# Two attentions and a mixture of experts on one core: the cosine shift in the score product, rotary halves on VectorE, idle products between chunks, narrow value units side by side

## The reference

```python
xn = _layernorm(x, axis=-1)
x = x + _L0_attn_ref(xn, Wq, Wk, Wv, g_scale) + _L0_ffn_ref(xn, g1, g2, wq, ...)

# _L0_attn_ref: 16 heads of 8 columns, cosine attention, no mask
q, k = _l2norm(q), _l2norm(k)
scores = g_scale * einsum('bhqd,bhkd->bhqk', q, k)
out = einsum('bhqk,bhkd->bhqd', softmax(scores), v)

# _L0_ffn_ref: 16 query heads, 4 key/value heads, rotary positions, causal
q = q * cos + _rotate_half(q) * sin        # k the same, then repeated
scores = where(causal, einsum('bhqd,bhkd->bhqk', q, k) / sqrt(8), -inf)
x = x + (softmax(scores) @ v) @ wo         # of the RMS-normed input
x = x + moe(rmsnorm(x))                    # 4 experts, top 2, hidden 384
```

## Time and profile before

| | us |
|---|---|
| median of 3 runs | 691.45 |
| lowest, highest | 690.83, 691.85 |
| profiled execution, its time | 691.39 |
| its span, first to last instruction | 689.7 |
| PE busy in the span | 631.6 |
| ACT busy | 479.7 |
| DVE busy | 361.7 |
| GpSimd busy | 110.5 |

### The profile page before, as it was taken

How to read it: one execution, slowest core, us unless ns; L and a number is a source line. 1 busy time by engine, 2 the same in 40 slices (tenths; PEclk the granted TensorE clock), 3 DMA queues, 4 the chain that set the end, 5 groups by cost and what they waited for, 6 DMA issues and landing times.

```text
span 689.7 us, 11207 instructions
## 1 busy us (share of the span) xinstructions
PE 631.6 (92%) x4138; PEld 284.3 (41%) x4138; DVE 361.7 (52%) x1037; ACT 479.7 (70%) x521; POOL 110.5 (16%) x257
## 2 busy tenths in 40 slices
PE   7758889999999999999999999999998789999996
PEld 6433333333333333333333333333333445566654
DVE  6586875565555555556455554553611434343333
ACT  1457868898898898889889889888997332222221
POOL 4488002102100200210210031021011200000000
PEclk8886999999999999999999999999999899999999
DMA  3002113214022120316302122030000000000000
GB/s 86 1 7 41 26 26 59 31 17 64 2 46 36 29 47 7 59 23 162 56 10 47 25 39 47 3 62 1 1 3 1 0 1 0 17 1 15 1 15 16
DMA packets 17525, 19.50 MB, mean 28 GB/s; under 512 B 6720, under 2 KB 14144, under 8 KB 17472
## 3 DMA queue, kind: packets, MB, share of 16 engines
q1 hardware_dynamic: 15072, 18.50, 15.2%
q10 hardware_dynamic: 2400, 0.30, 0.3%
HBM read 3.84 MB, written 1.05 MB: 7 GB/s over the span
## 4 chain that ended last, share of the span: by engine, by line
PE 74%; DVE 11%; ACT 8%; POOL 2%; issue 2%; DMA 1%; SPq 0%; DVEq 0%; ACTq 0%; POOLq 0%
PE ps L1197 25%; PE ps L1178 18%; PE ps L1292 6%; ACT probs L698 6%; PE ps L1278 6%; PE ps L1279 5%; PE ps L1123 5%; PE ps L1147 3%; DVE neg_piece L836 2%; DVE masked_scores L832 2%; DVE out_t L915 2%; PE ps L1140 1%; PE ps L1136 1%; DMA x_tok<-in_x 1%; PE ps L1089 1%
## 5 line engine op out<-in xcount | busy, mean ns | idle before, releaser
L698 ACT ACTIVATE probs<-ps,cos_shift 128x1024 f32<-128x1024 f32 x256 | 269.8, 1113 | 29.6 <-PE ps L1178 27.5
L701 ACT ACTIVATE probs<-ps 128x1024 f32<-128x1024 f32 (+2 forms) x160 | 144.7, 940 | 29.0 <-PE ps L1178 27.6
L832 DVE CUSTOM_DVE_ANT_0 masked_scores<-ps,mask_q 128x384 bf16<-128x384 f32 (+3 forms) x256 | 111.7, 488 | 73.7 <-PE ps L1123 73.0
L1197 PE MATMUL ps<-probs,v_cos_pad 128*32 128x512 f32 x1024 | 137.7, 610 | 0.0
L1178 PE MATMUL ps<-q_cos_t,k_cos_t 64*128 64x512 f32 x512 | 123.8, 482 | 5.0 <-ACT probs L698 3.9
L592 POOL TENSOR_SCALAR_AFFINE_SELECT probs<-probs 128x512 f32<-128x512 f32 x64 | 40.3, 635 | 404.2 <-ACT probs L701 404.2
L1178 PEld LDWEIGHTS ps<-q_cos_t,k_cos_t 64*128 64x128 f32 x512 | 48.2, 186 | 127.6 <-ACT probs L698 91.2
L739 ACT ACTIVATE probs<-ps 128x512 f32<-128x512 f32 x48 | 28.5, 597 | 96.3 <-PE ps L1279 84.9
L836 DVE TENSOR_REDUCE neg_piece<-ps 128x1 f32<-128x512 f32 x128 | 82.2, 684 | 22.8 <-PE ps L1123 22.8
L1197 PE MATMUL ps<-probs,v_causal_pad 128*32 128x512 f32 (+3 forms) x768 | 81.6, 498 | 0.3 <-POOL probs L592 0.3
L1123 PE MATMUL ps<-k_causal_t,q_causal_t 33*128 33x512 f32 (+3 forms) x384 | 64.4, 373 | 16.2 <-DVE neg_piece L836 9.0
(11 more groups left out here) (142 smaller groups left out, 458.1 us busy)
## 6 DMA issues: line engine op xcount, KB each, us to landing
q_causal_t<-parts_t_rope SPq DMA_DIRECT2D x64, 64.0 KB
q_cos_t<-parts_t_cos SPq DMA_DIRECT2D x56, 64.0 KB
k_cos_t<-parts_t_cos SPq DMA_DIRECT2D x28, 64.0 KB
k_cos_t<-parts_t_cos SPq DMA_DIRECT2D x56, 32.0 KB
parts_cos<-in_w SPq DMA_DIRECT2D x2, 768.0 KB, 5.7
x_tok<-in_x SPq DMA_DIRECT2D x4, 256.0 KB, 4.4
k_causal_t<-parts_t_rope SPq DMA_DIRECT2D x16, 64.0 KB
k_causal_t<-parts_t_rope SPq DMA_DIRECT2D x32, 32.0 KB
```

The source lines that it names most:

```text
L698: act.activation(step_probs(n), step_scores(n), ACT.Exp, bias=cos_shift[:, :])\
L701: act.activation(step_probs(n), step_scores(n), ACT.Exp).then_inc(probs_ready, 1)
L832: ins = dve.tensor_tensor_reduce(out=masked_scores[:, head % 2, at:at + keys], in0=scores, in1=mask_q[:, BANK - keys:BANK], scale=-1.0, sc ...
L1197: ins = pe.matmul(acc[32 * h:32 * h + 32, lo:], v, unit_probs(n)[:, h, lo:], start=j == 0, stop=True, skip_group_check=True)
```

## The change

1. *Cosine layout.* Each of the four heads gets 64 rows of its own in the keys (`k_cos_t` is twice as wide: two heads per half). 32 rows are the products; in two more, the queries hold the shift (rounded part and rest) and the keys hold 1. The exponential of the cosine steps has no bias any more. For the first group the constant rows are added when ACT and DVE copy the chosen rows (four copies each, three before); for later ones GpSimd fills the tiles once.
2. *Rotary halves.* DVE writes the second rotary halves, GpSimd no longer does.
3. *Unread products.* Six ahead of the projection of chunks 1, 2 and 3; six, not four, before the first scores.
4. *Narrow causal units.* The value unit of 256 columns moves one step later, to the step of the unit of 128 columns.
5. Score step 3 waits for DVE's copies (step 4 before).

```diff
@@ constants and the table of value units
-EARLY_WARM_UP, WARM_UP = 28, 4
+EARLY_WARM_UP, BETWEEN_CHUNKS, WARM_UP = 28, 6, 6
...
+    for n, (kind, half, j) in enumerate(UNITS * iters):
+        if kind == CAUSAL and j == half * CT + 2:
+
+            at[n] = at[n + 1]
     return at
...
-        k_cos_t = [sb(f"k_cos_t{i}", [P, SEQ]) for i in range(2)]
+        k_cos_t = [sb(f"k_cos_t{i}", [P, 2, SEQ]) for i in range(2)]
...
-        choose_q, choose_k = sb("choose_q", [P, 2, P]), sb("choose_k", [P, P])
+        choose = sb("choose", [P, 4, P])
+        rest_of_q, rest_of_k = sb("rest_of_q", [P, 1]), sb("rest_of_k", [P, 1])
@@ SP, lay_out_cos
                 for h in range(GROUP):
-                    first = cos_row(h)
-                    lay_out_key(signal, k_cos_t[it % 2], first, parts_t["cos"], COS_GROUP_COLS + h * HALF_COLS)
+                    first = h % 2 * HEAD_ROWS
+                    lay_out_key(signal, k_cos_t[it % 2][:, h // 2, :], first, parts_t["cos"],
+                                COS_GROUP_COLS + h * HALF_COLS)
@@ GpSimd
-            rotate(0)
-            for c in range(1, CHUNKS):
+            for c in range(CHUNKS):
                 rotate(c)
-                write_second_rope_halves(c - 1)
 
             pool.wait_ge(v_copied, 2)
             pool.wait_ge(v_read, 2)
             pad_cos_values(0)
-            write_second_rope_halves(CHUNKS - 1)
             pad_causal_values(0)
             clear_rows(1)
-            pool.memset(q_cos_t[1][:, :, :], 0.0).then_inc(rows_cleared, 1)
+            pool.wait_ge(cos_shift_steps, 9)
+            pool.tensor_copy(rounded(q_cos_t[1][:, :, :]), rest_of_q[:, :].unsqueeze(2).to_broadcast([P, 2, SEQ]))\
+                .then_inc(rows_cleared, 1)
+            pool.memset(k_cos_t[1][:, :, :], 1.0).then_inc(rows_cleared, 1)
@@ ACT
-            for i in range(3):
+            act.wait_ge(cos_shift_steps, 9)
+            act.wait_ge(choices_made, 14)
+            for i in range(4):
                 act.wait_ge(first_rows_in_psum, i + 1)
-                act.activation(first_rows(i, 0), ps[:, 5 + i, :], ACT.Copy).then_inc(first_rows_copied, 1)
+                act.activation(first_rows(i, 0), ps[:, 4 + i, :], ACT.Identity, bias=(rest_of_q, rest_of_k)[i // 2][:, :])\
+                   .then_inc(first_rows_copied, 1)
...
-                if ALL_STEPS[n % STEPS][0] == COS:
-                    act.activation(step_probs(n), step_scores(n), ACT.Exp, bias=cos_shift[:, :])\
-                       .then_inc(probs_ready, 1)
-                else:
-                    act.activation(step_probs(n), step_scores(n), ACT.Exp).then_inc(probs_ready, 1)
+                act.activation(step_probs(n), step_scores(n), ACT.Exp).then_inc(probs_ready, 1)
@@ DVE
+            def write_second_rope_halves(c):
+                rope_parts, rope_a = halves_of(c)[1], rope_a_of_chunk[c % 2]
+
+                dve.wait_ge(first_halves, 2 * c + 2)
+                dve.tensor_tensor(rounded(rope_parts[:, 1]), rope_a.rearrange("p (h d) -> p h d", d=HD), rope_parts[:, 0],
+                                   ALU.subtract).then_inc(rope_halves, 1)
...
             for c in range(1, CHUNKS):
                 read_projections(c)
                 write_second_cos_halves(c - 1)
+                write_second_rope_halves(c - 1)
                 normalise_units(c)
...
             write_second_cos_halves(CHUNKS - 1)
-            for i in range(3):
-                dve.wait_ge(first_rows_in_psum, 4 + i)
-                dve.tensor_copy(first_rows(i, 1), ps[:, 5 + i, :]).then_inc(other_rows_copied, 1)
+            write_second_rope_halves(CHUNKS - 1)
+            dve.wait_ge(choices_made, 14)
+            for i in range(4):
+                dve.wait_ge(first_rows_in_psum, 5 + i)
+                dve.tensor_scalar(first_rows(i, 1), ps[:, 4 + i, :], (rest_of_q, rest_of_k)[i // 2][:, :], None, ALU.add)\
+                   .then_inc(other_rows_copied, 1)
@@ PE
             def project_chunk(c):
                 pe.wait_ge(xt_ready, c + 1)
 
+                if c:
+                    warm_up(BETWEEN_CHUNKS, 6 + c % 2)
                 pe.wait_ge(rope_input_ready, c)
...
-                if n == FIRST_MAX_STEPS[0]:
-
-                    pe.wait_ge(other_rows_copied, 3)
+                if n == 3:
+
+                    pe.wait_ge(other_rows_copied, 4)
...
-                        keys, queries = k_cos_t[it % 2][rows, :], q_cos_t[it % 2][rows, a, :]
+                        keys, queries = k_cos_t[it % 2][rows, a, :], q_cos_t[it % 2][rows, a, :]
...
-            warm_up(WARM_UP, 4)
+            pe.wait_ge(q_and_k_copied, CHUNKS)
+            pe.wait_ge(rope_input_ready, CHUNKS)
+            warm_up(WARM_UP, 3)
```

More of the change, by code:

```diff
@@ L1073, in _, with warm_up @@
             pe.wait_ge(constants_made, 4)
+            def warm_up(products, wait_bank):
+                for _ in range(products):
+                    pe.matmul(ps[:, wait_bank, 0:P], ident[:, :], ident[:, :], start=True, stop=True)
             def transpose_xn(c):
```

72 lines of the change are left out of this document (41 added, 31 removed).

## The result

The changed kernel takes 687.08 us (median of 8 runs, 684.94 to 689.77) against 691.49 (8 runs, 689.62 to 692.81) beside it: a ratio of 0.9937, 95% interval 0.9914 to 0.996. It is 4.4 us faster; the forecast was 5.9. Run again with other kernels it gave 0.9932 (0.991 to 0.9954). The profiled execution took 688.20 us, span 686.4.

The account below looks back on a forecast made before the run. TensorE was taken to bound the kernel, ScalarE close behind. 691.39 us - 4.2 - 0.2 (shift: seven iterations, first) - 1.8 (narrow units) + 0.3 (start) = 685.5 us; range 681.5 to 690.

Parts of the forecast that it names:

- Change 1: Cosine half: the shift goes into the score product; exponentials fall from 1113 to 1026 ns, saving 0.6 us an iteration.
- S now follows M: Cosine half, two places: a score step (S) should start 0.24 to 0.35 us behind the row-maxima products (M).
- Rival (b): Middle iterations: TensorE waits for VectorE at its row-maxima products instead; saves only 1.9 us, total 689.5; chance 0.14.
- Rival (d): Cosine exponentials: the 87 ns belong to their place, not the operand; they stay at 1113 ns, total 689.9; chance 0.06.
- Change 2: Causal halves: the two narrow value units stand together, saving 0.25 us an iteration, 1.8 us in seven.
- the stretch: Causal half, from the value unit of 384 columns to the copy of the sums: 2.62 us before, 2.43 forecast.
- Change 3: The start, ahead of the first iteration: moved halves, unread products and copies together cost +0.3 us; bounds -2.5 and +3.
- what is won by 53.77: Start, ahead of step 3: 2.49 us plus a wait gone, less three moved halves, wins about 2 us.
- two halves, four copies and a signal: Start, from 54.3 us to step 3: remaining halves, copies and signal put step 3 at 60.2 to 60.6 us.
- (a): Start: TensorE less idle, clock stays at 2.4 GHz; 2.5 us gained instead of 0.3 lost, about 682.7; chance 0.18.
- (c): Start: VectorE's longer row delays step 3, TensorE idles and its clock falls; +8 us instead of +0.3, 693.2; chance 0.07.

Follow-up runs that it names:

- e1: Changed kernel with the cosine exponentials reading the bias operand again, all else as changed: 689.42 us, ratio 1.0003 to the kernel before.
- e12: e11 with step 3, not step 4, waiting for VectorE's three plain copies: 684.80 us, ratio 0.9909 to the kernel before.
- e11: e7 with the second rotary halves written by VectorE instead of GpSimd: 681.40 us, ratio 0.9862 to the kernel before.
- e4: Changed kernel without the six unread products ahead of chunks 1, 2 and 3: 685.75 us, ratio 0.9931 to the kernel before.
- e7: Kernel before with cosine exponentials' bias left out (shift not computed) and narrow causal units side by side: 683.04 us, ratio 0.9884 to the kernel before.
- e2: Changed kernel with the 256-column value unit back at its old step, narrow units apart: 688.93 us, ratio 0.9977 to the kernel before.
- e8: Kernel before with only the cosine exponentials' bias operand left out (shift not computed): 684.15 us, ratio 0.9902 to the kernel before.
- e3: Changed kernel with the second rotary halves back on GpSimd: 682.95 us, ratio 0.9893 to the kernel before.
- e10: Changed kernel with rotary halves on GpSimd, VectorE's four copies ahead of its last cosine half, and step 3's wait split: 679.86 us, ratio 0.9846.

## Why the forecast held, and where it didn't

**Change 1 was right**, in mechanism and size. The exponentials fell to 1024 ns in one form. I forecast 0.6 us an iteration; undone it costs 0.69, done alone it gives 0.64. S now follows M after 0.24 to 0.36 us. Rival (b) had its mechanism: the wait at 262.92 grew from 0.27 to 0.65 us, and PE's idle time for DVE ahead of M from 15.3 to 17.4 us in the whole run. But that is 2.1 us beside the 5.95 that the seven iterations lost, so its size is out. Rival (d) is out by e1, where the operand brings the 1113 ns back at the same place.

**Change 2 was right.** Forecast 0.25; 0.22 put in last, 0.30 taken out. In the profile the stretch is 2.53 us, not 2.43, so 0.09 of the forecast 0.19 shows there, and 0.09 in the other half, where 0.06 was forecast. That makes 0.18 of the 0.22 to 0.30; the rest no row places.

**Change 3 has the term that was mis-sized**: +0.3 us at step 3, measured +2.7 (2.63 by the chain). The step that failed is "I put what is won by 53.77 at about 2 us". In steps, counted from DVE's first reading of projections:

- Up to the reading of the last chunk 1.3 us were won (26.03 us before, 24.71 after). The moved halves took 1.27 us each there, not 0.85; the range's upper bound had used 1.4.
- From that reading to the end of the last normalising product it was 7.5 us before (48.81 to 56.30) and 9.6 after (47.60 to 57.17), 2.1 more. The moved half is 1.27 of it. L823 beside GpSimd's L540 is 1.1, and the small L806 beside GpSimd's L547 0.9 (1.36 us, where its like took 0.42); 1.2 come back, since the large product behind it takes 1.29 and not 2.53.
- 1.3 won and 2.1 lost make 0.8 us later, where I had 2 earlier. The difference, 2.8, is the whole miss.
- Behind that point the forecast held: two halves, four copies and a signal take 5.8 us (57.17 to 62.98); the forecast had 5.9 to 6.3. DVE's last copy is the releaser, as said.

I had weighed the rule of the Trainium skill ("SBUF — State Buffer", section "Who interferes with whom"), that a DVE instruction with two SBUF inputs and a GpSimd instruction reading SBUF exclude each other, against what GpSimd would lose. I didn't count what DVE would lose. By that rule DVE's row grows too, and it is DVE's row that step 3 waits for. The trace agrees for the moved half: it takes 1.34 us at 52.10, beside GpSimd's products, and 0.81 at 59.47, where GpSimd makes only short copies. Of the pair above the rule explains one, the one that comes second, and not both. The 64-column L806, a DVE instruction with one tile and one column as inputs, was held as well.

**The wait.** I priced the wait ahead of step 3 by its end alone, in the start's one sum. e12 shows that it costs by itself: 1.4 us in the chain, and 3.2 in the run time against e11, of which the part at half clock is not shown to be its own. e11 shows that without it the moved halves are free. From before to the changed kernel the chain adds up so: no bias -0.46, moved halves -0.12, the wait for three plain copies +1.37, then +1.84 up to 40.09. Of this 1.00 goes with the unread products (e4), which I had counted at nothing, and 0.84 with the fourth block and the additions. No run changed these alone, but the rows place them: DVE's copies start 36.32 us behind the mark both in e12 and in e4, and step 3 follows 1.93 us after that in e12 and 2.77 in e4.

Rivals (a) and (c) had the right subject. The clock from 55 to 70 us rose little (0.71 and 0.75, from 0.68), the first iteration took 64.42 and 63.02 us where it took 64.38, and the start as a whole got longer, so (a) didn't come. (c)'s mechanism is there, a late copy, PE idle, a slow first unit, but at a third of the size that it needed. The total came out 1.6 us above the forecast, and inside its range. In the profile, which is one of the longer executions, the miss is 2.6 us (3.3 won, not 5.9), and the start's chain is nearly all of it. That the median lies closer is luck of the executions, not of the sum.

## What to carry to other kernels

A wait costs from where it stands: ask of each one which instruction really needs the data, and put it there. Here one wait, one step too early, took some three of the eight microseconds that e7 had won; 1.4 of them are seen directly in the chain. When work moves from one engine to another and their instructions hold each other up, count the collisions on both, and compare starts from a mark behind the first clock-dependent stretch, or luck of 3 us hides the effect.

## What the runs showed of the hardware

- **Run times spread with the clock of the short stretches.** The iterations repeat within 0.4 us between profiles, and the totals of one kernel spread over up to 5 us (684.94 to 689.77). The first projections' 5.25 and 2.80 us are one source. The first iteration of the changed kernel (64.42 and 63.02 us from step 3) is another, and what follows the attention a third: 158.0 to 158.6 us in most profiles, 155.7 in those of e1, e2 and e8, where the stretch at half clock near 540 us is shorter.
- **The order decides who is held.** The large DVE product (L814) took 2.53 us beside GpSimd before. In the changed kernel a small one of 64 columns stands at that place and takes 1.36 instead of 0.42, and the large one takes 1.29. The last item is an exception, since both get longer.
- **Idle time ahead of a step doesn't tell the clock behind it.** PE is idle for 1.61 us ahead of step 3 in e3 and the clock stays full; it is idle for 0.39 in e7 and the clock is 0.55 from 60 to 68 us.
- **A gain in the chain needn't show.** e4's is 1.0 us shorter and its run time is the same, 0.9931 against 0.9932.
- **The pair L540 and L823** takes 1.1 us longer each in the five profiles with unread PE products ahead of the chunks and the halves on DVE, and doesn't in e4, e11 and e12, which lack the products, or in e3 and e10, which have the halves on GpSimd. The cause is open.
